# A graph attention and mixture-of-experts kernel: the GRU ahead of a transpose, exps in another order, the last iteration written out, and the adjacency's minus one moved to ACT

## The reference

```python
h = LN(x)
Wh = h @ W;  src = Wh @ a[:F];  dst = Wh @ a[F:]
att = softmax(where(adj > 0, leaky_relu(src + dst.T, 0.2), -9e15), axis=1)
h_prime = att @ Wh
gi = h_prime @ w_ih.T + b_ih;  gh = h @ w_hh.T + b_hh        # a GRU cell
r, z = sigmoid(i_r + h_r), sigmoid(i_z + h_z);  n = tanh(i_n + r * h_n)
x = x + (1 - z) * n + z * h
# then 16 experts, the two best for each row of LN(x), weighted by a softmax over the two:
logits = LN(x) @ gate_w + gate_b
x = x + sum over the two of p_e * ((silu(LN(x) @ w1[e]) * (LN(x) @ w2[e])) @ w3[e])
```

## Time and profile before

| | us |
|---|---|
| runs | 1275.27, 1278.59, 1282.17 (median 1278.59) |
| the profiled execution | 1278.3 |
| its span | 1276.5 |
| PE / PEld busy | 1154.3 / 1049.4 |
| DVE busy | 1047.4 |
| ACT busy | 775.3 |
| POOL busy | 348.1 |

### The profile page before, as it was taken

One profiled execution on the slowest core, in us unless ns is written; L12 is line 12 of the kernel. 1 busy time (PEld: TensorE's weight loads), 2 busy tenths in 40 slices (PEclk: granted clock), 3 DMA queues, 4 the chain that ended last, 5 costly groups with the idle time before them and its releaser, 6 DMA issues.

```text
span 1276.5 us, 25947 instructions
## 1 busy us (share of the span) xinstructions
PE 1154.3 (90%) x7574; PEld 1049.4 (82%) x7575; DVE 1047.4 (82%) x2485; ACT 775.3 (61%) x1125; POOL 348.1 (27%) x351
## 2 busy tenths in 40 slices
PE   5879999999999999999999994379999999999995
PEld 4568989898989898989898983268888888888884
DVE  7967888888888888889898964978888888888883
ACT  3576767676767676767676731036666666666662
POOL 2521010111111111111111000036555564555554
PEclk9879999999999999999999997569999999999998
DMA  8233333333434343434342200232444455435430
GB/s 239 36 56 50 63 70 65 69 69 67 72 62 76 60 79 59 80 58 80 59 79 58 47 26 20 75 108 47 100 101 98 95 144 141 121 68 141 94 50 8
DMA packets 61633, 98.64 MB, mean 77 GB/s; under 512 B 9472, under 2 KB 36096, under 8 KB 61536
## 3 DMA queue, kind: packets, MB, share of 16 engines
q0 software_dynamic: 33600, 52.49, 26.2%
q1 hardware_dynamic: 27936, 44.93, 10.8%
HBM read 213.18 MB, written 18.81 MB: 182 GB/s over the span
## 4 chain that ended last, share of the span: by engine, by line
PE 61%; DVE 18%; DMA 7%; issue 5%; ACT 5%; POOL 2%; DVEq 0%; POOLq 0%; ACTq 0%
PE bank L1252 13%; PE bank L1031 12%; PE bank L1266 8%; PE bank L1157 7%; DMA out<-ysc,cidx 7%; PE bank L1131 5%; PE bank L1132 5%; PE bank L1133 5%; PE bank L1162 4%; DVE pc L740 3%; ACT E L542 2%; ACT pc L488 2%; POOL rs L440 1%; DVE scr L792 1%; DVE scr L793 1%
## 5 line engine op out<-in xcount | busy, mean ns | idle before, releaser
L1131 PE MATMUL bank<-V,pc 128*128 128x258 f32 x1024 | 311.0, 304 | 3.8 <-DVE pc L740 3.8
L1132 PE MATMUL bank<-V,pc 128*128 128x258 f32 x1024 | 291.2, 284 | 0.0
L1133 PE MATMUL bank<-V,pc 128*128 128x258 f32 x1024 | 288.8, 282 | 0.0
L1252 PE MATMUL bank<-wup,xT 128*128 128x512 f32 x948 | 240.1, 402 | 0.9 <-DVE xT L978 0.9
L488 ACT ACTIVATE pc<-bank 128x512 fp32r<-128x512 f32 x256 | 151.6, 593 | 133.6 <-PE bank L1031 130.2
L740 DVE TENSOR_TENSOR pc<-bank,pc 128x512 fp32r<-128x512 f32 x256 | 175.6, 686 | 38.0 <-ACT pc L488 35.3
L1252 PEld LDWEIGHTS bank<-wup,xT 128*128 128x128 f32 x948 | 174.5, 191 | 35.6 <-DVE xT L978 1.3
L1131 PEld LDWEIGHTS bank<-V,pc 128*128 128x128 f32 x1024 | 193.9, 189 | 4.9 <-DVE pc L740 4.9
L1132 PEld LDWEIGHTS bank<-V,pc 128*128 128x128 f32 x1024 | 195.8, 191 | 0.0
L1133 PEld LDWEIGHTS bank<-V,pc 128*128 128x128 f32 x1024 | 195.7, 191 | 0.0
L973 DVE TENSOR_TENSOR wup<-wexp,wup 128x1024 fp32r<-128x1024 f32 x158 | 185.8, 1217 | 2.2 <-ACT wup L488 1.1
(11 more groups left out here) (159 smaller groups left out, 1641.4 us busy)
## 6 DMA issues: line engine op xcount, KB each, us to landing
wexp<-in_L_ffn_w SPq DMA_DIRECT2D x237, 512.0 KB
adjb<-in_adj POOLq DMA_DIRECT2D x128, 256.0 KB, 4.8
token_rows<-xrow SPq DMA_DIRECT2D x32, 130.0 KB, 2.3
E<-in_x SPq DMA_DIRECT2D x8, 512.0 KB, 9.0
xin<-in_x SPq DMA_DIRECT2D x32, 128.0 KB, 2.7
out<-xin SPq DMA_DIRECT2D x32, 128.0 KB, 1.7
xg<-token_rows,gidx POOLq DMA_INDIRECT x79
out<-ysc,cidx POOLq DMA_INDIRECT x79
```

The source lines that it names most:

```text
L1131: mm(acc[:, 0:VW], hi, V[:, j, 0, :], start=j == 0, stop=False)
L1132: mm(acc[:, 0:VW], hi, V[:, j, 1, :], start=False, stop=False)
L1133: ins = mm(acc[:, 0:VW], lo, V[:, j, 0, :], start=False, stop=j == T - 1)
L1252: ins = mm(acc[:, 0:HID], xT[:, r % WR, a, k * P:(k + 1) * P], wup[:, r % 2, n, b, k * HID:(k + 1) * HID], start=(k, a, b) == terms[0], st ...
```

## The change

1. PE: in body(i), gru(i) comes ahead of transpose_x2(i).
2. ACT: the logits of tile i + 1 come ahead of the xn2T copy; gate_exp goes from behind the exp of chunk 4 to ahead of the exp behind chunk 3, and n_tanh to ahead of the exp behind chunk 4.
3. less_one goes from DVE to ACT: an activation (Identity with a bias column of -1) behind the logits of each quarter, in the loop and for tile 0. A new constant mone is made by POOL, and the counts of constants are one higher.
4. The loop runs to T - 2; iteration T - 1 and the three behind it are written out for PE, ACT and DVE, in another order: the GRU and the xn2 transposes of body(T) stand ahead of the last two chunks.

```diff
+            def less_one(n, q):
+                act.wait_ge(s_adj[q], n * 16 + 16)
+                nc.scalar.activation(adjb[:, q, :], adjb[:, q, :], ACT.Identity, bias=mone[:, 0:1]).then_inc(s_am, 1)
...
                 if g % 2 == 1:
                     logits(0, g // 2)
+                    less_one(0, g // 2)
...
             def body(i):
-                if live(i, 3):
-                    act.wait_ge(s_t2, i - 2)
-                    act_copy(xn2T[:, :, :].rearrange("p k m -> p (k m)"), tp[:, 0:F]).then_inc(s_t2e, 1)
                 if i + 1 < T:
                     for q in range(Q):
                         logits(i + 1, q)
+                        less_one(i + 1, q)
+                if live(i, 3):
+                    copy_x2T(i)
                 for c in range(CPT):
                     if live(i, 0):
                         chunk_hi(i * CPT + c + 2)
+                    if c == 3 and live(i, 3):
+                        gate_exp(i)
+                    if c == 4 and live(i, 2):
+                        n_tanh(i)
                     if 1 <= c < 1 + Q and i + 1 < T:
                         weights(i + 1, c - 1)
...
-                if ahead:
-                    less_one(i + 1, 0)
-                    less_one(i + 1, 1)
                 if live(i, 1):
                     combine(i - 1)
                     remake_xn(i - 1)
                 if ahead:
                     mask_logits(i + 1, 0)
-                    less_one(i + 1, 2)
                     mask_logits(i + 1, 1)
-                    less_one(i + 1, 3)
                     mask_logits(i + 1, 2)
...
             def body(i):
+                if live(i, 2):
+                    gru(i)
                 if live(i, 3):
                     transpose_x2(i)
-                if live(i, 2):
-                    gru(i)
```

The end, written out, for DVE, ACT and PE (last is (T - 1) * CPT):

```diff
+            combine(T - 2); remake_xn(T - 2); chunk_lo(last + 2); gru_logits(T - 1); chunk_lo(last + 3)
+            route_top(T - 1); gru_n(T - 1); chunk_lo(last + 4); route_weights(T - 1); chunk_lo(last + 5)
+            gru_out(T - 1); hT_lo(T - 1); chunk_lo(last + 6); norm2(T - 1); chunk_lo(last + 7)
+            gru_logits(T); route_top(T); gru_n(T); combine(T - 1); remake_xn(T - 1); route_weights(T)
+            hT_lo(T); gru_out(T); norm2(T); gru_logits(T + 1); route_top(T + 1); gru_n(T + 1)
+            route_weights(T + 1); gru_out(T + 1); norm2(T + 1); route_top(T + 2); route_weights(T + 2)
...
+            copy_x2T(T - 1); chunk_hi(last + 2); chunk_hi(last + 3); rz_tanh(T - 1); chunk_hi(last + 4)
+            gate_exp(T - 1); n_tanh(T - 1); chunk_hi(last + 5); copy_hT(T - 1); chunk_hi(last + 6)
+            chunk_hi(last + 7); copy_x2T(T); rz_tanh(T); gate_exp(T); n_tanh(T); copy_hT(T)
+            copy_x2T(T + 1); rz_tanh(T + 1); gate_exp(T + 1); n_tanh(T + 1); copy_x2T(T + 2); gate_exp(T + 2)
...
+            gru(T - 1); transpose_x2(T - 1); chunk(0); gate(T - 1); chunk(1); chunk(2); transpose_h(T - 1)
+            chunk(3); chunk(4); chunk(5); transpose_x2(T); gru(T); gate(T); chunk(6); chunk(7)
+            transpose_h(T); gru(T + 1); transpose_x2(T + 1); gate(T + 1); transpose_x2(T + 2); gate(T + 2)
```

More of the change, by code:

```diff
@@ L119, in gnn_moe @@
         mhalf = sb("mhalf", [P, 1], F32, gs)
+        mone = sb("mone", [P, 1], F32, gs)
         dmx = sb("dmx", [P, 2, Q], F32, gs)
@@ L319, in wait_apart @@
                 eng.wait_ge(semaphore, v)
-        CONSTS = 8
+        CONSTS = 9
         @block.sync
@@ L393, in _ @@
             nc.gpsimd.memset(mhalf[:], -0.5).then_inc(s_const, 1)
-            pool.wait_ge(s_const, 2)
+            nc.gpsimd.memset(mone[:], -1.0).then_inc(s_const, 1)
+            pool.wait_ge(s_const, 3)
             nc.gpsimd.affine_select(out=ident[:], in_=ident[:], compare_op=ALU.not_equal, fill=1.0, base=0,
@@ L413, in _ @@
                            allow_small_or_imprecise_dtypes=True).then_inc(s_const, 1)
-            pool.wait_ge(s_const, 7)
+            pool.wait_ge(s_const, 8)
             nc.gpsimd.affine_select(out=before[:], in_=before[:], compare_op=ALU.is_gt, fill=0.0, base=0,
@@ L584, in copy_hT, with copy_x2T @@
                 act_copy(hT[:, 0, :, :].rearrange("p k m -> p (k m)"), tp[:, :]).then_inc(s_hT, 1)
+            def copy_x2T(i):
+                act.wait_ge(s_t2, i - 2)
+                act_copy(xn2T[:, :, :].rearrange("p k m -> p (k m)"), tp[:, 0:F]).then_inc(s_t2e, 1)
             def gate_exp(i):
@@ L608, in body @@
                         copy_hT(i)
[L609 to L614, removed]
-                body(i)
+            for i in range(T - 1):
+                body(i)
+            last = (T - 1) * CPT
+            copy_x2T(T - 1)
+            chunk_hi(last + 2)
+            chunk_hi(last + 3)
+            rz_tanh(T - 1)
+            chunk_hi(last + 4)
+            gate_exp(T - 1)
+            n_tanh(T - 1)
+            chunk_hi(last + 5)
+            copy_hT(T - 1)
+            chunk_hi(last + 6)
+            chunk_hi(last + 7)
+            copy_x2T(T)
+            rz_tanh(T)
+            gate_exp(T)
+            n_tanh(T)
+            copy_hT(T)
+            copy_x2T(T + 1)
+            rz_tanh(T + 1)
+            gate_exp(T + 1)
+            n_tanh(T + 1)
+            copy_x2T(T + 2)
+            gate_exp(T + 2)
             def copy_slot_xT(s, r, st):
@@ L715, in _ @@
             V_.tensor_copy(wrep[:, :, :], wa[:, :, 1:2].broadcast_to([P, KB, P])).then_inc(s_wa, 1)
-            def less_one(n, q):
-                dve.wait_ge(s_adj[q], n * 16 + 16)
-                V_.tensor_scalar(adjb[:, q, :], adjb[:, q, :], 1.0, None, ALU.subtract).then_inc(s_am, 1)
             def mask_logits(n, q):
@@ L839, in _ @@
                     statistics(g + 2)
-                if g >= 5:
-                    less_one(0, g - 5)
                 scale_values(g - 1)
@@ L844, in _ @@
                     mask_logits(0, g - 6)
-            less_one(0, 3)
             mask_logits(0, 2)
@@ L893, in body @@
                             weights_lo(n)
-            for i in range(LAST):
+            for i in range(T - 1):
                 body(i)
+            last = (T - 1) * CPT
+            combine(T - 2)
+            remake_xn(T - 2)
+            chunk_lo(last + 2)
+            gru_logits(T - 1)
+            chunk_lo(last + 3)
+            route_top(T - 1)
+            gru_n(T - 1)
+            chunk_lo(last + 4)
+            route_weights(T - 1)
+            chunk_lo(last + 5)
+            gru_out(T - 1)
+            hT_lo(T - 1)
+            chunk_lo(last + 6)
+            norm2(T - 1)
+            chunk_lo(last + 7)
+            gru_logits(T)
+            route_top(T)
+            gru_n(T)
+            combine(T - 1)
+            remake_xn(T - 1)
+            route_weights(T)
+            hT_lo(T)
+            gru_out(T)
+            norm2(T)
+            gru_logits(T + 1)
+            route_top(T + 1)
+            gru_n(T + 1)
+            route_weights(T + 1)
+            gru_out(T + 1)
+            norm2(T + 1)
+            route_top(T + 2)
+            route_weights(T + 2)
             dve.wait_ge(s_x1s, T * 16)
@@ L1092, in weights_step @@
                 ins.then_inc(s_wtr, 1)
-            pe.wait_ge(s_const, 3)
+            pe.wait_ge(s_const, 4)
             transpose_xn(0, 0)
@@ L1208, in body, with chunk @@
                         transpose_h(i)
-            for i in range(LAST):
+            for i in range(T - 1):
                 body(i)
+            last = (T - 1) * CPT
+            def chunk(c):
+                transpose_weights(last + c + 2)
+                accumulate(T - 1, c)
+            gru(T - 1)
+            transpose_x2(T - 1)
+            chunk(0)
+            gate(T - 1)
+            chunk(1)
+            chunk(2)
+            transpose_h(T - 1)
+            chunk(3)
+            chunk(4)
+            chunk(5)
+            transpose_x2(T)
+            gru(T)
+            gate(T)
+            chunk(6)
+            chunk(7)
+            transpose_h(T)
+            gru(T + 1)
+            transpose_x2(T + 1)
+            gate(T + 1)
+            transpose_x2(T + 2)
+            gate(T + 2)
             pe.wait_ge(s_row, T)
```

## The result

The changed kernel is slower: median 1299.53 us (1294.13 to 1302.90) against 1277.99 us, ratio 1.0167, 95% interval [1.0136, 1.0197]. The forecast was 1291 us, between 1274 and 1304. The profiled execution took 1298.7 us, its span 1296.9 us against 1276.5.

The account below looks back on a forecast made before the run. The prediction took a loop through PE, ACT's copy and DVE up to hT_lo (21.55 us) as the bound, passing to ACT's queue before the gate (22.06); 1278.3 + 7 + 14.3 - 8.3 = 1291.3 us, range 1274 to 1304.

Parts of the forecast that it names:

- What ends the head's wait: PE's wait of about 1.2 us before each iteration's head ends with DVE's hT_lo, not the xrow the profile names.
- GRU first, exps reordered, both 0: PE's GRU ahead of the xn2 transposes, and ACT's gate_exp and n_tanh ahead of exps: each worth 0.
- the ring: Chain closing an iteration: before, PE, ACT's copy, DVE to hT_lo, 21.55 us; after, ACT's queue to the gate, 22.06.
- less_one on ACT: Four activations, one every 1.04 us, delay the gate: 9.95 plus 12.11 us, period 22.06, +0.51; +14.3 us over 28 iterations.
- The second path, 0.2 us shorter: Later exps on ACT delay the next head; the gate could be at 9.7 us, covered by ACT's 9.95.
- The relief on DVE worth nothing: DVE loses about 1.4 us of subtractions an iteration, outside the 5.43 us that close the loop: worth 0.
- The start: Before the steady loop: +2 us until the value scale, +2 iteration 0, +2.5 iteration 1, +0.7 iteration 2; +7 (4 to 10).
- The tail: Last iteration written apart, with the GRU ahead of the last two chunks: -8.3 us (-9 to -6).
- The hidden wait: Rival: eight activations fit in 7.8 us or the gate has slack, so DVE's path stays; 1275 us, chance 0.14.
- DVE's relief pays: Rival: DVE's queue as a whole bounds the loop, so PE's 1.05 us at each head goes; 1248 us, chance 0.08.
- Pairs without overlap: Rival: waits between logits and less_one on ACT break overlap, 8 x 1.14, period 22.86; 1313 us, chance 0.12.
- The sum: Whole kernel: 1278.3 + 7 + 14.3 - 8.3 = 1291.3 us, forecast 1291.

Follow-up runs that it names:

- x2_first: Changed kernel with the xn2 transposes ahead of the GRU again in PE's loop; 1296.24 us, period 22.08 us.
- hTlo_early_dve: less_on_dve with hT_lo moved behind gru_out, ahead of a chunk_lo and norm2, in DVE's loop; 1255.86 us, ratio 0.9850, period 21.08 us.
- less_on_dve: Changed kernel with less_one back on DVE at its old places, the other parts kept; 1270.32 us, ratio to before 0.9949, period 21.53 us.
- old_exps: Changed kernel with gate_exp and n_tanh back behind the fourth exp in ACT's loop; 1294.94 us, period 22.08 us.
- gate_later: Changed kernel with the gate's matmuls behind chunk 1 instead of chunk 0 in PE's loop; 1298.18 us, mean period 21.89 us.
- early_two_on_act: hTlo_early_dve with less_one of quarters 0 and 1 on ACT from tile 4; 1238.65 us, ratio 0.9694, period 20.41 us.
- start_on_dve: Changed kernel with less_one on DVE for tiles 0 to 3 and on ACT from tile 4; 1286.74 us, period 22.09 us.
- three_on_act: start_on_dve with quarter 0 also on DVE from tile 4, leaving ACT three less_ones an iteration; 1272.3 us, period 21.53 us.
- hTlo_early_act: Changed kernel (less_one on ACT) with hT_lo behind gru_out in DVE's loop; 1320.5 us, period 23.62 or 22.08 us.
- only_less_on_act: Kernel before with only less_one moved to ACT, behind each quarter's logits; 1384.13 us, period 24.63 us.

## Why the prediction was right, and where its sizes were off

**What ends the head's wait: right.** The forecast put it down to hT_lo where the profile named xrow. With the GRU first, the profile names hT_lo itself; in x2_first nothing changes; moving hT_lo alone (hTlo_early_dve against less_on_dve) takes the wait away. The row of xrow in the kernel before, which ends at 441.04, is 0.7 us ahead of PE's 441.74, and not 0.6 as I had read it:

```profile
440.63 0.41 DVE L807 TENSOR_SCALAR xrow<-xin,mv,rs 128x256 f32<-128x256 f32 x1 [0.69 <-POOL rs L440]
```

**GRU first, exps reordered, both 0: right.** x2_first and old_exps leave the period at 22.08. In less_on_dve, where ACT is not the ring, all the orders together are worth 0.02 us an iteration.

**less_one on ACT: right in place and size.** Forecast was an activation every 1.04 us, 9.95 us from the last chunk's transposes to the gate and 12.11 from there on, period 22.06. The trace has 1.14 us each, 1.04 apart, 9.87 (458.63 to the gate at 468.50), 12.22 and 22.09; the two parts are off by 0.1 us in opposite directions, so that the sum fits to 0.03 is partly luck. The price for which the trace of before had no row, bf16 on ACT, is a mean of 1137 ns over 128. The estimate of 1.13 us worked out from the Trainium skill ("ScalarE: Activation LUTs", What ACT_TABLE_LOAD costs), which gives one cost for fp32 and bf16, agrees. The advice of the Trainium skill to use VectorE for adds ("ScalarE: Activation LUTs", Rules for kernel authors) held for the change, 0.34 us against 1.04 on a ring, and not for early_two_on_act, where ACT's time was free.

**The second path, 0.2 us shorter: right.** gate_later took the gate's wait away and gained 0.2.

**The relief on DVE worth nothing: right** for the change. It becomes worth 0.34 us a quarter once hT_lo is early.

**The start: mis-sized,** 7 us forecast, 13.0 found. By ACT's and PE's marks: 4.3 until the first exp (67.22 to 71.54) where I had 2, 2.0 in iteration 0 as forecast, 4.4 in iteration 1 for 2.5, and 2.3 in iteration 2 for 0.7. The three that failed failed in different ways.

In iteration 1 the wait was right: the third chunk's chunk_lo comes 4.41 us behind the transposes ahead of it, for 1.94 before, the 2.5 of the forecast. The other 1.9 us are durations that I had kept: PE works slower behind that wait. Windows of the kernel after, in iteration 1:

```profile
105.00:112.00 7.00, 6.78 (x56) 6.41 (x54) 4.37 (x8) 6.21 (x8) 0.53 (x1) 1.00 0.09 4
112.00:118.00 6.00, 1.66 (x7) 1.66 (x8) 3.76 (x10) 4.20 (x6) 1.34 (x3) 0.69 0.81 119
118.00:125.00 7.00, 7.00 (x49) 7.00 (x49) 2.48 (x4) 5.82 (x8) 0.25 (x1) 0.78 0.30 46
```

PE, stopped for the third chunk, is busy 1.66 of 6 us, and its clock is 0.69 and 0.78 of full where it was 1.00 throughout before. Its first transposes behind that take 1.05 us instead of 0.60:

```profile
119.09 1.05 PE L1088 MATMUL bank<-ident,E 128*128 128x128 f32 x4
```

In iteration 2 the clock was 1.00 throughout, so there it was waiting that I had too short. The head of iteration 3 waited 2.44 us for hT_lo, for 1.02 before (1.4 of the 2.3), and the third chunk's transposes stood 2.50 us behind the second's, for 1.88 before (0.6):

```profile
152.98 3.07 PE L1214 MATMUL bank<-wT,hT 128*128 128x512 f32 x12 [2.44 <-DVE hT L797]
```

Until the first exp, the wait for the first adjacency quarter was 1.21 us on ACT, not 3, and the last less_one stood between logits and mask as forecast. But a group of 16 matmuls on PE ahead of it took 3.41 us, where it took 1.85 before, at a granted clock of 0.53 (56 to 60 us), and DVE waited long at the end:

```profile
56.73 3.41 PE L1109 MATMUL bank<-wa,xnT 128*128 128x2 f32 x16
```

```profile
69.89 1.23 DVE L755 CUSTOM_DVE_ANT_0 E<-E,adjb 128x1024 f32<-128x1024 f32 x1 [6.01 <-ACT adjb L543]
```

The clock is down at times in this stretch of the kernel before too (0.57 from 48 to 52 us, 0.68 from 56 to 60), and no run separates clock from waiting in it. The start also varies by itself: the GRU of iteration 2 came at 127.8 to 135.2 in four kernels alike up to there (after, gate_later, old_exps, x2_first), and at 119.1 to 122.1 in four with less_one on DVE there (before, less_on_dve, start_on_dve, three_on_act). Part of the 13.0 is therefore this execution's own.

**The tail: mis-sized,** -8.3 forecast, -6.6 found, for the reason that stood there as the other end. PE in the kernel after:

```profile
788.70 0.44 PE L1088 MATMUL bank<-ident,xrow 128*128 128x128 f32 x2 [0.95 <-DVE xrow L838]
...
799.89 4.61 PE L1214 MATMUL bank<-wT,hT 128*128 128x512 f32 x12 [1.41 <-DVE hT L797]
...
817.77 1.03 PE L1302 MATMUL bank<-pick,before 128*128 128x512 bf16 x2 [1.89 <-DVE xrow L860]
```

The last GRU still ran at a mixed clock (0.50 from 801 to 803 us, 1.00 from 804), 6.1 us to DVE's read of it at 805.96, where I took 4.5. With 6.3 the sum had been -6.5.

**The rivals.** The hidden wait fell with 22.09 us, and three_on_act shows what it would have needed: one activation fewer. That DVE's relief pays fell with the change and came true under another order. Pairs without overlap fell with starts 1.04 us apart.

**The sum.** The profiled execution, 1298.7 us, lies 7.4 above the sum of 1291.3: 6.0 in the start, 1.7 in the tail, 0.3 in the loop, and 0.6 less in the stage behind. The start's 13.0 lies outside its own bounds of 4 to 10; the range held because the loop and the tail came near or within theirs.

## What to carry to other kernels

A move of work between engines is priced by the ring that closes the loop and not by busy shares: four activations cost 0, 0.5 or 3.1 us an iteration here, depending on what stood in front of them and how many there were. Find first what the head of the loop really waits for: where two semaphores were waited for, the profile named the one whose work ended 0.7 us too early, and the two or three lines that moved hT_lo were worth more than the change. When a wait of the matmul engine grows, don't take the durations of what stands behind it for granted: carry a second value at the lower clock, as a bound, for waits of one length had both clocks behind them here.

## What the runs showed of the hardware

Two things I had not expected. PE's granted clock can fall behind a short wait in an otherwise full loop, but the length of the wait doesn't tell when. In hTlo_early_act the gate waits 1.50 to 1.52 us in 27 iterations; in 21 the clock is 0.57 to 0.73 in the 4 us behind it, which costs 1.5 us each, and in six it stays at 1.00. In gate_later every second head waits 1.7 us, and the clock stays at 1.00 behind all of them:

```profile
466.13:470.13 4.00, 4.00 (x22) 3.46 (x23) 3.96 (x9) 4.00 (x5) 0.57 (x1) 1.00 0.01 2
```

In only_less_on_act 29 heads wait about 2 us, and behind 13 of them the clock is 0.57 to 0.67; the period stays near 24.63 all the same, for the ring there runs through ACT and not through the matmuls that are slowed. And a loop over several engines can settle into a period of two iterations: 22.26 and 21.51 us in turn in gate_later, with the head's wait at 1.70 and 0.96 us.
